# Reordering the pair-product reads in a fused DLRM tower: read and merge first in two engines' slots, dense columns before GpSimd's product, last features in two parts

## The reference

```python
e = stack([tbl_f[ids[:, f]] for f in range(26)], axis=1)        # 512 x 26 x 64
x = layer_norm(r_dense_t @ Wd.T)                                 # 512 x 128
y = layer_norm(einsum('bnd,ed->bne', e, Ws))                     # 512 x 26 x 128
y = layer_norm(einsum('bne,pn->bep', y, Wsi))                    # 512 x 128 x 32
T = concatenate([x[:, None, :], swapaxes(y, 1, 2)], axis=1)      # 512 x 33 x 128
Z = einsum('bnd,bmd->bnm', T, T)[:, TRIL_I, TRIL_J]              # 528 pairs a sample
z = layer_norm(Z @ Wl.T) * (arange(512) < 384)
h = relu(concatenate([z, r_dense_t], axis=1) @ W_top1 + b_top1)
h = relu(h @ W_top2 + b_top2)
out = h @ W_top3                                                 # 512 x 1
```

## Time and profile before

| | |
|---|---|
| median of 3 runs | 185.95 us (185.07 to 186.01) |
| profiled execution | 184.83 us, of which the span is 182.9 us |
| busy: PE, DVE, POOL, ACT | 83%, 66%, 60%, 47% of the span |
| mean granted TensorE clock | 0.981 of full speed |
| chain that ended last, by engine | PE 41%, POOL 19%, DVE 12%, ACT 12%, issue 12% |

### The profile page before, as it was taken

One profiled execution on the slowest core, in us unless ns is written; L12 is line 12 of the kernel. 1 busy time (PEld: TensorE's weight loads), 2 busy tenths in 40 slices (PEclk: granted clock), 3 DMA queues, 4 the chain that ended last, 5 costly groups with the idle time before them and its releaser, 6 DMA issues.

```text
span 182.9 us, 3485 instructions
## 1 busy us (share of the span) xinstructions
PE 151.1 (83%) x1378; PEld 108.9 (60%) x1378; DVE 121.6 (66%) x251; ACT 86.1 (47%) x224; POOL 109.5 (60%) x110
## 2 busy tenths in 40 slices
PE   0588968797199968699897699999967988899994
PEld 0323556764184855545694578377855964559992
DVE  6768608489968488485869894939799597900330
ACT  3014232246374586984543545264353556551242
POOL 2787778777777877777778777777875040300000
PEclk9999999699969999999999999999999999999999
DMA  5701642524111111111111111111111000000000
GB/s 139 269 14 39 213 111 58 189 40 138 24 22 32 22 22 32 29 25 28 22 28 26 22 29 31 24 29 27 29 22 32 0 0 4 0 4 0 4 0 0
DMA packets 5728, 8.14 MB, mean 44 GB/s; under 512 B 2357, under 2 KB 3279, under 8 KB 5712
## 3 DMA queue, kind: packets, MB, share of 16 engines
q0 software_dynamic: 3328, 3.41, 9.7%
q1 hardware_dynamic: 1664, 3.65, 6.2%
q10 hardware_dynamic: 720, 0.85, 1.4%
HBM read 7.91 MB, written 0.00 MB: 43 GB/s over the span
## 4 chain that ended last, share of the span: by engine, by line
PE 41%; POOL 19%; DVE 12%; ACT 12%; issue 12%; DMA 1%; POOLq 1%; ACTq 0%
POOL G L299 18%; PE ps_tail L1031 6%; PE ps_tail L1047 5%; PE ps_y L982 4%; PE ps_z L989 4%; PE ps_z L1078 4%; PE ps_tail L1057 3%; DVE V L740 3%; PE ps_y L1089 3%; PE ps_tail L944 2%; PE ps_gq L954 2%; DVE V L753 2%; ACT gt L386 2%; PE ps_ut L972 2%; ACT sd L404 2%
## 5 line engine op out<-in xcount | busy, mean ns | idle before, releaser
L299 POOL DMA_INDIRECT G<-in_table_dram,idx x104 | 105.5, 1014 | 34.6 <-issue 31.4
L972 PE MATMUL ps_ut<-S,G 128*128 128x192 f32 (+4 forms) x128 | 22.6, 324 | 1.1 <-DVE G L726 1.1
L982 PE MATMUL ps_y<-ut,wcg 64*128 64x512 f32 x64 | 18.1, 641 | 5.2 <-ACT ut L395 5.1
L972 PEld LDWEIGHTS ps_ut<-S,G 128*128 128x128 f32 x128 | 20.9, 207 | 1.6 <-DVE G L726 1.3
L400 ACT ACTIVATE sq<-V 128x1024 f32<-128x1024 f32 x15 | 15.9, 1062 | 12.3 <-DVE V L740 12.3
L747 DVE TENSOR_REDUCE var<-sq 128x32 f32<-128x1024 f32 x15 | 18.3, 1219 | 4.8 <-ACT sq L400 4.8
L740 DVE TENSOR_TENSOR V<-ps_y,bias_y 128x512 f32<-128x512 f32 x32 | 20.5, 682 | 0.6 <-PE ps_y L982 0.4
L989 PEld LDWEIGHTS ps_z<-V 128*64 128x64 f32 x448 | 14.3, 136 | 9.6 <-issue 6.2
L954 PE MATMUL ps_gq<-eye,G 128*128 128x128 f32 x52 | 9.8, 306 | 11.8 <-DMA G<-in_table_dram,idx 11.6
L989 PE MATMUL ps_z<-V 128*64 128x67 f32 x448 | 16.2, 224 | 1.8 <-ACT zx L462 1.6
L751 DVE RECIPROCAL r<-sd 128x32 f32<-128x32 f32 x13 | 4.6, 353 | 18.8 <-ACT sd L404 18.8
(11 more groups left out here) (155 smaller groups left out, 248.1 us busy)
## 6 DMA issues: line engine op xcount, KB each, us to landing
G<-in_table_dram,idx POOLq DMA_INDIRECT x104, 2.5
w1z<-in_w_z_dram SPq DMA_DIRECT2D x1, 768.0 KB, 4.1
wl<-in_wl_blocks_dram SPq DMA_DIRECT2D x1, 768.0 KB, 4.4
dns<-in_dense_t_dram ACTq DMA_DIRECT2D x1, 512.0 KB, 4.4
w1d<-in_w_d_dram SPq DMA_DIRECT2D x1, 512.0 KB, 5.3
wl<-in_wl_blocks_dram SPq DMA_DIRECT2D x1, 512.0 KB, 3.6
w2s<-in_w_dram SPq DMA_DIRECT2D x1, 512.0 KB, 3.7
wrow<-in_wsi_rows_dram SPq DMA_DIRECT2D x1, 208.0 KB
```

The source lines that it names most:

```text
L299: pool.indirect_dma_start(G[:, n // NC, j, g, :], None, table, bass.IndirectOffsetOnAxis(ap=idx[:, k:k + 1], axis=0)).then_inc(gathered[n ...
L972: mm = pe.matmul(ps_ut[:, chunk % 2, col:col + width], G[:, gp, j, :, :].rearrange("p g d -> p (g d)"), S[:, j, :, :].rearrange("p s q -> ...
L982: pe.matmul(ps_y[:, g, :], wcg[64 * g:64 * g + 64, :], ut[64 * g:64 * g + 64, :], start=True, stop=True).then_inc(y_ps, 1)
```

## The change

- ScalarE's slot does `z_evacuate(n-3)` first, ahead of `gt_copy(n)`, `deviation2(n-2)` and, in c=0 slots, `f_scale`; also in the slot of chunk 14, written out singly.
- VectorE's slot does `z_merge(n-3)` ahead of `normalise2(n-2)`; the gathers' pacing waits swap their first two steps to match.
- In the slot of chunk 15 VectorE does both `x_slots` first, ahead of `root2`, which starts GpSimd's product.
- The fourth column block of the last features goes to another PSUM bank (`ps_y[:, 1]`); its completion is signalled apart from that of the first three. ScalarE squares in two parts. TensorE's order becomes: first half of `last_layer1`, sum of squares, second half of `last_layer1`, all of group 2's `layer1`.

```diff
@@ gpsimd, steps @@
-                every = [(v_ready, n - 1), (z_merged, n - 2), (q_used, n + 1), ...
+                every = [(z_merged, n - 2), (v_ready, n - 1), (q_used, n + 1), ...
@@ scalar @@
             def last_f_squares(gp):
-                act.activation(f_sq[:, :, :], tail2, ACT.Square).then_inc(f_sq_ready, 1)
+                act.activation(f_sq[:, 0:LLIVE, :], tail2[:, 0:LLIVE, :], ACT.Square)
+                act.wait_ge(f_ps, gp + 2)
+                act.activation(f_sq[:, LLIVE:LC, :], last_f_ps, ACT.Square).then_inc(f_sq_ready, 1)
...
             def slot(n):
                 gp, c = divmod(n, NC)
+                z_evacuate(n - 3)
                 gt_copy(n)
                 deviation2(n - 2)
                 if c == 0 and gp > 1:
                     f_scale(gp - 2)
-                z_evacuate(n - 3)
                 ut_copy(n - 1)
@@ vector, slot @@
-                normalise2(n - 2)
                 if n >= 3:
                     z_merge(n - 3)
+                normalise2(n - 2)
@@ vector, chunk 15 @@
+            x_slots(n - 1)
+            x_slots(n)
             root2(n - 2)
             variance1(n)
-            x_slots(n - 1)
-            x_slots(n)
             scale_rows(n)
@@ tensor @@
-                        mm = pe.matmul(tail2[:, lc, :], wl[...], ...
+                        mm = pe.matmul(tail2[:, lc, :] if lc < LLIVE else ps_y[:, 1, 0:GRAN], wl[...], ...
-                mm.then_inc(f_ps, 1)
+                    if lc >= LLIVE - 1:
+                        mm.then_inc(f_ps, 1)
...
             last_project_pairs(gp)
-            layer1(gp - 1, ocs=range(0, 2))
+            last_layer1(gp, range(0, 2))
             last_sum_squares(gp)
-            last_layer1(gp, range(OC1))
-            layer1(gp - 1, ocs=range(2, OC1))
+            last_layer1(gp, range(2, OC1))
+            layer1(gp - 1)
             last_layer2(gp)
```

More of the change, by code:

```diff
@@ L182, in dlrm_tower @@
         last_y_ps = ps_z[0:1, 0, 0:GRAN]
+        last_f_ps = ps_y[:, 1, 0:GRAN].unsqueeze(1)
         ld_ids, ld_wc, ld_ws, ld_wd, ld_pm, ld_sm, ld_s, ld_x, ld_w1z, ld_w1d, ld_w2, ld_gs = [
@@ L282, in steps @@
             def steps(n, count):
-                every = [(v_ready, n - 1), (z_merged, n - 2), (q_used, n + 1), (var1_ready, n + 1), (y_sb, 2 * n - 1), (y_sb, 2 * n),
+                every = [(z_merged, n - 2), (v_ready, n - 1), (q_used, n + 1), (var1_ready, n + 1), (y_sb, 2 * n - 1), (y_sb, 2 * n),
                          (g_scaled, n + 1), (var2_ready, n)]
@@ L1088, in last_project_pairs @@
                     for k in range(KB):
-                        mm = pe.matmul(tail2[:, lc, :], wl[:, k, lc * P:(lc + 1) * P], zb[:, k, at] if k < PB else zx[:, at],
+                        mm = pe.matmul(tail2[:, lc, :] if lc < LLIVE else ps_y[:, 1, 0:GRAN], wl[:, k, lc * P:(lc + 1) * P], zb[:, k, at] if k < PB else zx[:, at],
                                        start=(k == 0), stop=(k == KB - 1))
-                mm.then_inc(f_ps, 1)
+                    if lc >= LLIVE - 1:
+                        mm.then_inc(f_ps, 1)
             def last_sum_squares(gp):
```

## The result

The changed kernel takes 183.69 us (median of 6, 182.75 to 185.83) against 186.05 us (median of 6, 185.07 to 187.35): ratio 0.9846, 95% interval 0.9804 to 0.9887. Measured again later with other runs of both: 183.9 against 187.23 us, ratio 0.9797 (0.9762 to 0.9832). The ratios leave out slow executions, so they are not quotients of the medians. The forecast was 184.3 us, a gain of 1.6 us; the gain is 2.4 and 3.3 us by the medians, 2.9 and 3.8 us by the two ratios. So the sign was right and the size too small by a factor of 1.5 to 2.4.

The account below looks back on a forecast made before the run. Bounds: GpSimd's gathers decide chunk starts, a loop over all engines paces slots, TensorE fills the end. 1.2 (read and merge) + 0.4 (dense columns) + 0 (last features) = 1.6 us; 185.95 - 1.6 = 184.3 us, range 183.2 to 185.7.

Parts of the forecast that it names:

- Gain of parts 1 and 2: 2.0 - 0.8 = 1.2 us: ScalarE's read and VectorE's merge moved first: at most 2.0 us by chunk 14's embedding, less 0.8 for later gathers.
- Parts 1 and 2 in a group, from chunk 8 to chunk 11: Slots of one group: 0.43 us in the c=0 slot, then 0.4 and 0.42 in the next two, 1.25 together.
- How they come about: c=0 slot: ScalarE's earlier read brings `ut_copy`, and with it the embedding, 0.43 us earlier; VectorE's merge gives 0.4 in c=1.
- The rival in which `normalise2` is held by the merge: VectorE's queue: the merge's data comes too late and holds `normalise2` by up to 0.50 us, gain 0; no separate chance.
- What is gained before chunk 10 I count as nothing: Slots before chunk 10: gain counted as 0, since chunk 10's transposes, like chunk 14's, wait for the DMA.
- 2.0 us is the most: Chunk 14's embedding, at 138.99, can come at 137.0 at the earliest with its data landing at 134.39.
- I take +0.8: Chunk 14's gathers land 0.8 us later because moved multiplies hold gathers; bounds -0.8 to +3.6, average +1.6.
- The pacing waits do not bind: GpSimd's gathers follow one another every 1.25 us with only issue ahead, so swapping two pacing waits costs nothing.
- Part 3: Chunk 15's slot: `x_slots` copies moved into VectorE's wait, multiply of `G` still held; gain 0.4 us, bounds 0 to 1.23.
- Part 4: Last features in two parts: TensorE issues the same matmuls in another order; 0 us, bounds -0.3 to +0.6.
- larger gain: Gathers lose nothing, or chunk 15's `G` multiply is not held, and merges before chunk 10 count: 2.4 to 3.2 us; chance 0.12.
- It holds `gt_copy`: ScalarE: late products make `z_evacuate` hold `gt_copy`, gain 0 from that move, 185.1 to 185.9 us; counted within a 0.27 chance.

Follow-up runs that it names:

- after: Profiled execution of the whole changed kernel: 184.11 us, span 182.3 us; the profiled execution of the kernel before took 184.83 us.
- after_3: The whole change measured again against the kernel before: 183.9 against 187.23 us, ratio 0.9797.
- e_no_tail: The whole change without the last features in two parts, against the kernel before: 183.42 against 186.83 us, ratio 0.9832.
- e_slots: Only ScalarE's `z_evacuate` and VectorE's `z_merge` moved first, against the kernel before: 184.37 against 186.25 us, ratio 0.9911.
- e_no_x: The whole change without moving the two `x_slots` copies, against the kernel before: 183.93 against 186.83 us, ratio 0.9855.
- b_plain_2: Kernel before with gathers from chunk 8 replaced by plain DMAs, against the kernel before: 186.62 against 187.23 us, ratio 0.9971.
- a_plain_2: Changed kernel with gathers from chunk 8 replaced by plain DMAs, against the kernel before: 183.77 against 187.23 us, ratio 0.9808.
- e_act: Only ScalarE's `z_evacuate` moved first, VectorE's merge where it was, against the kernel before: 187.26 against 186.25 us, ratio 1.0058.
- e_tail_2: Only the last features in two parts, measured again, against the kernel before: 186.67 against 186.83 us, ratio 0.9996.
- e_xslots: Only the two `x_slots` copies of chunk 15's slot moved first, against the kernel before: 186.28 against 186.25 us, ratio 0.999.
- e_tail: Only the last features in two parts, against the kernel before: 185.94 against 186.25 us, ratio 0.9962.
- e_dve_2: Part 2 alone: only VectorE's `z_merge` first and pacing waits swapped, against the kernel before: 191.96 against 187.23 us, ratio 1.0245.

## Why the prediction was right in sign and short in size

The step that failed is the one that gave "Gain of parts 1 and 2: 2.0 - 0.8 = 1.2 us". It counted too few slots, it took as a cap the landing of chunk 14 in one execution, and it set the gathers' loss against the changed kernel alone. The stretch from chunk 5 to chunk 15 (last column of the table) measures parts 1 and 2 by themselves. Without gathers they give 83.93 - 80.98 = 2.95 us. With gathers they give 2.3, 2.4 and 2.95 in the three late-starting traces of the changed kernel (after, after_3, e_no_tail), against the trace before; in the two early-starting ones, -0.2 (e_slots) and 0.95 (e_no_x).

- *Parts 1 and 2 in a group, from chunk 8 to chunk 11: right.* Forecast 0.43 in the c=0 slot and 0.4 + 0.42 in the next two, 1.25 us. Without gathers (b_plain_2 and a_plain_2): chunk 8 to 9 takes 8.46 and 8.06, chunk 9 to 11 takes 16.48 and 15.52: 0.40 + 0.96 = 1.36. The same in the last group: 0.39 + 0.97.
- *How they come about: half right.* I gave the c=0 slot's gain to part 1 alone, since `ut_copy` released the embedding. e_act shows no gain there: chunk 8 to 9 takes 88.02 to 96.54 = 8.52 us. `ut_copy` was one of two waits; behind it stood `zn`, through VectorE. The rival in which `normalise2` is held by the merge is what part 2 alone does.
- *"What is gained before chunk 10 I count as nothing": wrong.* In the traces after, chunk 10's transposes still wait for the DMA, yet chunk 9 to 11 takes 15.51 us, as much as without gathers (15.52). There was room behind them: where no DMA holds chunk 10 (e_no_tail), its projection waits 1.23 us for VectorE's `G`. In e_no_x the data came later still (a wait of 2.35 us), and chunk 9 to 11 took 17.52. Counted in, the sum is 2 x 1.36 = 2.7 us instead of 2.1. Chunk 5 to 8 adds another 0.2: 25.60 us without the change (b_plain_2), 25.38 with it (a_plain_2). Together that is the 2.95.
- *"2.0 us is the most", and "I take +0.8" for the landing of chunk 14: wrong in what it was set against.* As a size the 0.8 was not bad: chunks 7 to 15 take 66.0 and 65.9 us in the two traces after and 65.3 without gathers, so 0.6 us are lost there. But the cap, from a landing at 134.39, belongs to the one execution that I had read, and the kernel before loses at the gathers too: chunk 9 to 11 takes 16.44 in its trace, but 17.34 in e_tail_2 and 17.06 in e_xslots, which order these slots as it does.

  How much the gathers cost depends on the multiplies that they meet and on how far their stream is ahead when chunk 5 starts. The last gather of chunk 5 ends 3.7 to 4.3 us before chunk 5's transposes in four traces (before, e_slots, e_no_x, e_tail_2), 4.5 to 5.4 us before them in six (after, after_3, e_no_tail, e_act, e_xslots, e_tail). The four are those in which chunk 5 starts at 60.5 to 60.7 us, with a granted clock of 0.80 to 0.84 between 50 and 60 us; with 0.67 to 0.74 it starts at 61.9 to 62.7, in seven traces; two lie between (e_dve_2 with 0.78 at 61.50, a_plain_2 with 0.79 at 61.39). The rows that show the clock, from the busy time by stretch (the clock is the third number from the end), before and after:

```profile
50.00:60.00 10.00, 10.00 (x52) 6.45 (x53) 6.93 (x14) 5.69 (x16) 7.87 (x8) 0.84 0.14 26
```

```profile
50.00:60.00 10.00, 8.92 (x29) 6.29 (x30) 5.81 (x12) 5.14 (x12) 7.87 (x8) 0.69 0.14 27
```

  That the clock is the cause is not shown, and it can't be all of it. Of the 2.01 us by which chunk 5 starts later after than before, 1.28 are there already at chunk 4's transposes (49.80 and 51.08), which the DMA released in both:

```profile
49.80 1.09 PE L954 MATMUL ps_gq<-eye,G 128*128 128x128 f32 x4 [4.45 <-DMA G<-in_table_dram,idx]
```

```profile
51.08 1.12 PE L957 MATMUL ps_gq<-eye,G 128*128 128x128 f32 x4 [5.89 <-DMA G<-in_table_dram,idx]
```

  e_slots is the counterpart: its trace caught the same early start as the one before (60.70, clock 0.83), and in it the gathers took the whole gain, chunk 15 starting at 144.84 against 144.43. Its waits for the data in the slots of chunks 12 and 14:

```profile
119.90 0.66 PE L954 MATMUL ps_gq<-eye,G 128*128 128x128 f32 x4 [0.57 <-DMA G<-in_table_dram,idx]
...
135.75 0.48 PE L954 MATMUL ps_gq<-eye,G 128*128 128x128 f32 x1 [2.97 <-DMA G<-in_table_dram,idx]
```

  So for an execution like the one that I had read the forecast of 1.2 us was even high (-0.2 and 0.95); for the median it was low, because I subtracted a gain worked out in an early-starting execution from a median over executions of which, by the traces, more start late. With the late starts the sum is 2.95 - 0.6 + 0.4 = 2.75 us where the kernel before loses nothing to the gathers, and up to 0.9 more where it loses as in e_tail_2: 2.75 to 3.65, against 2.4 to 3.8 measured.
- *"The pacing waits do not bind": right in the execution read, not in general.* In e_act, e_tail, e_tail_2 and e_xslots the gathers wait 0.6 us for VectorE's multiply of `V` near 126 us, and 1.0 us near 134 us; in the traces of the whole change none does. The transposes of chunks 13 to 15 did not wait for their data in these four, so the waits cost nothing there.
- *Part 3: right.* 0.4 forecast, 0.35 to 0.44 in the traces, with the multiply of `G` held as forecast (0.83 us long, ending 0.42 after GpSimd's product; in e_xslots 0.82 long). The rule of the Trainium skill ("SBUF — State Buffer", section "Who interferes with whom") that such a multiply and GpSimd's product shut each other out gave the right one of two prices.
- *Part 4: right.* 0 forecast; 25.6 us from chunk 14's pair products to the end in the traces of before, after, e_tail, e_tail_2, e_no_tail and e_no_x.
- *Of the rivals,* "larger gain" is nearest to what happened, by the merges before chunk 10 that it named, not by gathers that lose nothing; that the kernel before loses as well stood in none. "It holds `gt_copy`" did not occur in the slots of chunks 8 to 15. In chunk 7's slot `gt_copy` starts 1.61 us behind the transposes' start instead of 1.15, within the bounds given for it; chunk 7 to 8 takes 9.69 us instead of 9.62.

What stays open: why the stream of gathers is further ahead in some executions, how often each kind occurs, and with it why the first two measurements of the whole, 0.9846 and 0.9797, lie 0.9 us apart.

## What to carry to other kernels

Before a gain worked out in one profiled execution is taken from a median, check that the execution is like the median: here it had reached one early chunk up to 2.2 us before the others, and with that start the gathers took more of the changed kernel's gain. A loss that the change meets must also be looked for in the kernel before; only the difference counts. When two engines hand a buffer on, try both ends together: here each move alone made the kernel slower, by 1.1 and 4.6 us, the two together faster by 1.7. And a wait at a chunk's transposes is no bound as long as what stands behind them waits for another engine anyway.

## What the runs showed of the hardware

Most gathers that start under a multiply are held until it is over. In 11 traces I looked at the 1052 gathers after 16 us. 121 of them took over 1.0 us instead of 0.94, and 119 of these had started inside a VectorE multiply of `V` or `G` by `r`, with both operands in SBUF, and ended 0.80 to 0.83 us after that multiply's end. Another 70 started inside such a multiply and were not held: 51 in its last 0.17 us, where there is next to nothing left to wait for, and 19 within 0.04 us behind its start, which took their 0.94 us while it ran on. The prediction's "waits for its end" leaves these 19 out. The Trainium skill ("SBUF — State Buffer", section "Who interferes with whom") counts such a multiply as harmless to descriptor generation; by these runs it delays a gather that starts under it by up to 1.05 us (1.99 instead of 0.94).
